# Grouped attention: queries taken transposed from the product, scores over 128 rows of cosine and sine parts, VectorE's bias and maximum ahead of the next tile's rotation

## The reference, cut to what matters

```
def _apply_rope(x, cos, sin):
    x1, x2 = (x[..., :d // 2], x[..., d // 2:])
    c1, c2 = (cos[..., :d // 2], cos[..., d // 2:])
    s1, s2 = (sin[..., :d // 2], sin[..., d // 2:])
    return concatenate([x1 * c1 - x2 * s1, x1 * s2 + x2 * c2], axis=-1)
```

## Time and profile before

| | us |
|---|---|
| time, median of 3 runs (lowest to highest) | 1008.42 (1007.82 to 1012.86) |
| time of the profiled execution | 1005.3 |
| its span, first to last instruction | 1003.5 |
| TensorE busy | 899.9 (90%) |
| VectorE busy | 669.8 (67%) |
| ScalarE busy | 420.8 (42%) |
| GpSimd busy | 375.3 (37%) |
| mean granted clock of TensorE | 0.968 |

### The profile page before, as it was taken

How to read it: one execution, slowest core, us unless ns; L and a number is a source line. 1 busy time by engine, 2 the same in 40 slices (tenths; PEclk the granted TensorE clock), 3 DMA queues, 4 the chain that set the end, 5 groups by cost and what they waited for, 6 DMA issues and landing times. The chain is left out here.

```text
span 1003.5 us, 17466 instructions
## 1 busy us (share of the span) xinstructions
PE 899.9 (90%) x5857; PEld 642.7 (64%) x5864; DVE 669.8 (67%) x1572; ACT 420.8 (42%) x1134; POOL 375.3 (37%) x279
## 2 busy tenths in 40 slices
PE   2899989999889995868899979999999949999997
PEld 2687744444478873744378647777777727778786
DVE  5899968889689988876377698787767531222221
ACT  2566641000146555752455336565655512122222
POOL 1776403333476732506545503333333430111111
PEclk9999999999899997987999999999999969999999
DMA  6100079999400007202356392311110149534200
GB/s 210 59 1 0 1 199 306 319 313 311 170 1 1 0 1 190 87 0 92 112 169 203 91 332 73 112 54 51 51 51 26 43 157 318 190 110 141 93 12 20
DMA packets 87259, 117.17 MB, mean 117 GB/s; under 512 B 12464, under 2 KB 75949, under 8 KB 86781
## 3 DMA queue, kind: packets, MB, share of 16 engines
q1 hardware_dynamic: 77455, 88.15, 29.1%
q10 hardware_dynamic: 4408, 15.46, 4.4%
q0 software_dynamic: 5328, 12.70, 3.5%
HBM read 68.08 MB, written 50.16 MB: 118 GB/s over the span
## 5 line engine op out<-in xcount | busy, mean ns | idle before, releaser
L1016 PE MATMUL psum<-m_W,lnT 128*128 128x512 f32 x256 | 114.2, 598 | 0.7 <-DVE acc L928 0.7
L410 POOL TENSOR_TENSOR prob<-prob,a_rden 128x1232 f32<-128x1232 f32 x30 | 67.5, 2249 | 58.4 <-DVE a_rden L506 58.4
L1016 PEld LDWEIGHTS psum<-m_W,lnT 128*128 128x128 f32 x256 | 47.2, 190 | 59.0 <-issue 56.5
L2907 ACT ACTIVATE prob<-psum,x_b 128x320 f32<-128x320 f32 x64 | 33.7, 527 | 117.1 <-PE psum L2963 117.1
L2574 PE MATMUL psum<-g_VW,pT 128*128 128x256 f32 (+1 forms) x320 | 72.5, 382 | 1.6 <-ACT pT L2461 1.5
L1001 POOL TENSOR_TENSOR m_masked<-m_rel,m_mrow 128x1232 f32<-128x1232 f32 x16 | 41.8, 2614 | 82.9 <-DMA masked_bias<-m_masked 62.0
L2769 POOL DMA_INDIRECT out_x<-x_yt,x_X x20 | 19.8, 991 | 135.3 <-DVE x_yt L2846 135.3
L2574 PEld LDWEIGHTS psum<-g_VW,pT 128*128 128x128 f32 (+1 forms) x320 | 59.5, 190 | 11.2 <-issue 3.7
L2232 POOL TENSOR_TENSOR g_qr<-g_t 128x1024 f32<-128x1024 f32 x15 | 35.4, 2359 | 71.1 <-DVE g_t L2305 71.1
L2239 POOL TENSOR_TENSOR prob<-prob,g_rden 128x1232 f32<-128x1232 f32 x15 | 33.7, 2247 | 67.6 <-DVE g_rden L2340 67.6
L2524 PE MATMUL psum<-g_Wq,lnT 128*128 128x512 f32 x128 | 58.0, 596 | 0.7 <-ACT lnT L2435 0.7
(11 more groups left out here) (464 smaller groups left out, 2235.6 us busy)
## 6 DMA issues: line engine op xcount, KB each, us to landing
routed_rows<-hole SPq DMA_DIRECT2D x8, 2210.0 KB, 33.5
masked_bias<-m_masked ACTq DMA_DIRECT2D x16, 616.0 KB, 7.5
g_bias<-masked_bias SPq DMA_DIRECT2D x16, 616.0 KB, 3.8
m_xb<-routed_rows SPq DMA_DIRECT2D x39, 130.0 KB
m_rel<-in_rel_bias ACTq DMA_DIRECT2D x8, 616.0 KB, 9.6
expert_rows<-hole SPq DMA_DIRECT2D x1, 4680.0 KB, 32.4
g_early_w<-in_L_ffn_w SPq DMA_DIRECT2D x8, 512.0 KB, 4.6
g_early_w<-in_L_ffn_w SPq DMA_DIRECT2D x4, 1024.0 KB, 5.9
```

The source lines that it names most:

```text
L410: nc.gpsimd.tensor_tensor(heads(c.prob[b]), heads(c.prob[b]), rden[b][:, :].unsqueeze(2).to_broadcast([P, H, SK]), ALU.mult).then_inc(norm ...
L1016: last = nt.matmul(c.ps[p][:, :], c.lnT[b][:, k * P:(k + 1) * P], W[:, k, p * 512:(p + 1) * 512], start=(k == 0), stop=(k == KC - 1))
```

## The change

*Queries.* The weights are now the stationary operand and the normalized tile the moving one: 16 matmuls of 128 columns, and the queries come out transposed, the 128 numbers of two heads in the rows and the tokens in the columns. Neither `q_transpose` nor `qT_copy` is left.

*Rotation.* VectorE multiplies the transposed queries with tables (`turn`) whose rows are the 64 numbers of a head and whose columns are positions. Cosine part and sine part aren't added: they are put in the two halves of 128 rows of `turned`, one block of 128 columns for each head. Four instructions of 64 rows, two of which write to the other half of the rows than they read.

*Scores.* One matmul a head, over all 128 rows, so that the contraction adds the two parts: the moving operand `KB` has the keys in rows 0 to 63 and the keys with their halves exchanged in rows 64 to 127, 77 columns, without zeros.

*Softmax.* The maximum is taken in two halves of 8 heads; the exponentials of all 16 heads are single ones with their sums, so the shift and the sums on VectorE are gone. GpSimd's addition is gone.

*Orders.* VectorE: shift(t) now stands ahead of rope(t+1). TensorE: output is cut into three parts among the transposes; `lnT(t+3)` instead of t+2; two banks for the probabilities' transposes; queries of tile 1 in banks 5 and 6, all others in 3 and 4. The additions of experts' results, layer norms' groups, and router pieces stand at other tiles (`COLLECT_AT`, `VARIANCE_AT`, `NORM_GROUPS`). Three small transfers come later in SP's queue.

```
-    c.gC, c.gSn = sb(c, "g_cos", [P, S // P, DH]), sb(c, "g_sin", [P, S // P, DH])
-    c.gKB = sb(c, "g_KB", [P, B, G, 2, SK])
+    c.gC, c.gSn = sb(c, "g_cos", [P, DH]), sb(c, "g_sin", [P, DH])
+    c.gTurn = [sb(c, f"g_turn{u}", [P, S]) for u in range(2)]
+    c.gKB = sb(c, "g_KB", [P, B, G, SK])
...
         def rope(i, u):
+            q = c.psall[:, q_bank(i) * 512:q_bank(i) * 512 + 1024].rearrange("p (m n) -> p m n", n=P)
+            to = turned[i % 2][:, :].rearrange("p (m u n) -> p m u n", u=2, n=P)
+            n0 = i % HALF * P
+            own, other = slice(u * DH, (u + 1) * DH), slice((1 - u) * DH, (2 - u) * DH)
+            if u == 0:
+                dve.wait_ge(s["q_ps"], i + 1)
+                wait(dve, s["s_ps"], i - 1)
+            for rows_, table in ((own, turn[0]), (other, turn[1])):
+                last = nv.tensor_tensor(to[rows_, :, u, :], q[own, :, :],
+                                        table[own, n0:n0 + P].unsqueeze(1).to_broadcast([DH, HB // 2, P]), ALU.mult)
+            if u == 1:
+                last.then_inc(s["roped"], 1)
...
         def shift(t):
+            dve.wait_ge(s["added"], t + 1)
+            nv.reduce_max(mx[b][:, halves[0]], p[:, halves[0]], AX, negate=True).then_inc(s["mx_ok"], 1)
             dve.wait_ge(s["s_used"], t + 1)
-            links(nv.reduce_max(c.mx[:, :], p, AX, negate=True))
-            nv.tensor_tensor(p[:, plain], p[:, plain], c.mx[:, plain].unsqueeze(2).to_broadcast([P, HB - FUSED, SK]),
-                             ALU.add).then_inc(s["shifted"], 1)
+            nv.reduce_max(mx[b][:, halves[1]], p[:, halves[1]], AX, negate=True).then_inc(s["mx_ok"], 1)
...
+        for t in range(NT - 1):
+            if t == HALF + 1:
+                centred()
+            if t in (4, 8):
+                inverse(NORM_OF[t + 3])
+            shift(t)
+            rope(t + 1, 0)
+            rope(t + 1, 1)
             route(t)
+            if t > 0:
+                finished(t - 1)
+            collect(t)
+            places(t)
+            divisors(t)
...
         def queries(i):
             pe.wait_ge(s["lnT_ok"], i + 1)
+            if i >= 2:
+                pe.wait_ge(s["roped"], 1 if i == 2 else i)
+            for m in range(HB // 2):
+                to = c.psall[:, q_bank(i) * 512 + m * P:q_bank(i) * 512 + (m + 1) * P]
                 for k in range(KC):
+                    last = nt.matmul(to, Wq[:, k, m * P:(m + 1) * P], c.lnT[i % 2][:, k * P:(k + 1) * P],
+                                     start=(k == 0), stop=(k == KC - 1))
...
         def scores(t):
+            pe.wait_ge(s["roped"], t + 1)
             wait(pe, s["s_used"], t)
-            for m in range(HB // 2):
+            for h in range(HB):
+                o = h // HPB * 512 + h % HPB * SK
+                last = nt.matmul(c.psall[:, o:o + SK], turned[t % 2][:, h * P:(h + 1) * P], KB[:, t // HALF, h // G, :],
...
+            if t > 0:
+                prob_transpose(t - 1, 0)
+                prob_transpose(t - 1, 1)
+                output(t - 1, 0)
+                prob_transpose(t - 1, 2)
+                if t < NT:
+                    route(t)
+                output(t - 1, 1)
+                if 2 <= t and t + 3 < NT:
+                    lnT(t + 3)
+                output(t - 1, 2)
+                back(t)
+                if t + 2 < NT:
+                    queries(t + 2)
```

More of the change, by code:

```diff
@@ L2098, in _ @@
         for b in range(B):
[L2099 removed]
+            pe.wait_ge(s["kr_ok"], 3 * (b + 1))
             for g in range(G):
@@ L2330, in residual, with divisors @@
-        def residual(i, b):
+            nv.reduce_max(mx[b][:, halves[1]], p[:, halves[1]], AX, negate=True).then_inc(s["mx_ok"], 1)
+        def divisors(t):
+            b = t % 2
+            wait(dve, s["p_ok"], t - 1)
+            dve.wait_ge(s["exp_ok"], t + 1)
+            nv.reciprocal(rden[b][:, :], den[b][:, :]).then_inc(s["rd_ok"], 1)
+            if t == NT - 1:
+                p = heads(c.prob[b])
+                dve.wait_ge(s["rd_ok"], t + 1)
+                for h in halves:
+                    nv.tensor_tensor(p[:, h], p[:, h], rden[b][:, h].unsqueeze(2).to_broadcast([P, HB // 2, SK]),
+                                     ALU.mult).then_inc(s["p_last"], 1)
@@ L2475, in route @@
                 logits_copy(c, r, 0, c.ps[0]).then_inc(s["r_lgT_ok"], 1)
-        def step(t, q):
-            b = q % 2
+        deviation(0)
+        layer_norm(0)
+        lnT_copy(0)
+        deviation(1)
+        na.activation(spare[:, :], c.ones[:, 0:1], ACT.Exp)
+        for i in range(1, 4):
+            layer_norm(i)
+            lnT_copy(i)
+        for t in range(NT):
             if t == HALF + 7:
@@ L2566, in output @@
-        def output(i, b):
-            if i == 0:
-                pe.wait_ge(s["r_rw_ok"], KC)
-            wait(pe, s["x_ok"], i)
-            for j in range(NB):
-                if j % 4 == 0:
-                    pe.wait_ge(s["pT_ok"], i * 3 + (j // 4 + 1))
-                w = P if j < NB - 1 else LASTB
-                last = nt.matmul(bank_y[:, 0:D], c.pT[b][0:w, j * P:(j + 1) * P], VW[0:w, i // HALF, j, :],
+            if i == NT - 1 and u < 2:
+                pe.wait_ge(s["p_last"], u + 1)
@@ new lines, in prob_transpose @@
+            if u == 0:
+                wait(pe, s["pT_ok"], i * 3)
+            elif u == 1:
+                pe.wait_ge(s["lnT_ok"], min(i + 4, NT))
+            else:
+                pe.wait_ge(s["pT_ok"], i * 3 + 1)
+            for j in range(4 * u, min(4 * u + 4, NB)):
+                w = P if j < NB - 1 else LASTB
+                last = nt.transpose(ring[u % 2][0:w, (j % 4) * P:(j % 4 + 1) * P],
+                                    c.prob[i % 2][:, j * P:j * P + w], c.ident[:, :])
+            last.then_inc(s["pT_ps"], 1)
@@ L2575, in output @@
+        def output(i, u):
+            if u == 0:
+                wait(pe, s["x_ok"], i)
+            pe.wait_ge(s["pT_ok"], i * 3 + (u + 1))
+            for j in range(4 * u, min(4 * u + 4, NB)):
+                w = P if j < NB - 1 else LASTB
+                last = nt.matmul(bank_y[:, 0:D], c.pT[i % 2][0:w, j * P:(j + 1) * P], VW[0:w, i // HALF, j, :],
                                  start=(j == 0), stop=(j == NB - 1))
-            last.then_inc(s["y_ps"], 1)
+            if u == 2:
+                last.then_inc(s["y_ps"], 1)
@@ L2609, in banks_read @@
                 pe.wait_ge(s["r_pre_read"], 1)
-        def step(t, q):
-            b = q % 2
+        lnT(0)
+        queries(0)
+        lnT(1)
+        queries(1)
+        lnT(2)
+        for t in range(NT + 1):
             banks_read(t)
-            if inside(t):
-                scores(t, b)
+            if t < NT:
+                scores(t)
             if t == 0:
-                pe.wait_ge(s["r_w_in"], 16)
-                for k in range(KC):
-                    last = nt.matmul(bank_y[:, 0:RW], c.ones[:, :], r.rw[:, k, :], start=(k == 0), stop=(k == KC - 1))
-                last.then_inc(s["r_sum_ps"], 1)
-            if t == HALF + 7:
+                queries(2)
+                lnT(3)
+            if t == NT - 1:
                 pe.wait_ge(s["r_lnT_ok"], ROUTED[2][0])
                 pe_logits(c, r, 1, c.ps[3]).then_inc(s["r_lg_ps"], 1)
+                pe.wait_ge(s["pT_ok"], (NT - 2) * 3)
+                keep_warm(c, ring[0], 6)
             if t == NT:
```

418 lines of the change are left out of this document (168 added, 250 removed).

## The result

The changed kernel takes 1060.52 us (median of 4 runs, 1058.03 to 1064.84) beside 1008.49 us (1007.82 to 1012.86) for the kernel before: a ratio of 1.0511, 95% interval 1.0465 to 1.0557. The direction and most of the 52 us were forecast; the time lies 15.5 us above the 1045 and just outside the range. The profiled execution has a span of 1057.8 us, 54.3 more than the earlier trace rows.

What follows compares the result with a forecast made beforehand. A serial TensorE-VectorE loop was to bind, 15.2 us a tile against 12.9: scores(15) 32.0 us later, +1.6 for that block, +3 at the end, +37 on 1005.3, 1042; plus 3.1 to the median, 1045 us, range 1022 to 1060.

Steps and rivals of the forecast that it cites:

- TensorE's passes: TensorE per tile: queries 32 passes, 3.65 us (+0.2); scores 32 passes of 77 columns at 0.117 us, 3.74 us (+1.64).
- The rival of serial loads and passes: Queries and scores: weight loads and passes don't overlap, 7.0 and 5.6 us a tile, 83 us more, 1128 us; chance 0.02.
- VectorE's half-height instructions: Rotation on VectorE: 64-row instructions cost the same as 128-row ones, 1.14 us start to start; four take 4.65 us.
- The ring: Serial loop per tile: scores, VectorE's bias, maxima and next tile's rotation, then TensorE's queries; 15.2 us against 12.9.
- bias with maxima: VectorE between scores and rotation: bias 1.03 + 0.50 us, maxima 0.70 + 0.70 us, 2.93 us together.
- the hand-over back: From the end of VectorE's rotation to the start of TensorE's next queries: 0.05 us.
- the first rival: The ring doesn't bind; TensorE's own 13.8 us do, 1.4 us a tile less, 20 us less: 1025 us; chance 0.08.
- The clock: Attention stage: granted clock stays at 1.00 (2.4 GHz) despite TensorE's idle time; priced at nothing.
- The start: First tiles: rotation of tile 0 from about 585.24, scores(0) at about 591.5, scores(1) at 603.1, then 15.2 us a tile.
- The end: From scores(15): the block itself +1.6 us; last output done 17.5 us after the scores instead of 14.4, +3 us.

Runs made afterwards that it cites:

- the run with the missed terms mended: Changed kernel with unused TensorE passes before scores(1) and the last transposes, lnT(4) behind scores(2), router copies ahead of exponentials: 1047.2 us, ratio 1.0383.
- the first: Changed kernel with VectorE's rotation of tile t+1 put ahead of bias and maximum of tile t: 1051.7 us, ratio 1.0380.
- the second: Changed kernel with TensorE issuing scores(t+1) ahead of queries(t+2) from tile 2 on: 1080.4 us, ratio 1.0640.
- the third: Changed kernel with rotation ahead of bias and maximum, third probabilities copy ahead of exponentials, four groups of unused TensorE passes: 1047.2 us, ratio 1.0391.

## Why the prediction missed

*TensorE's passes: right.* Queries 3.65 us, as worked out. Scores 3.53 us from start to start (703.34 to 706.87), 0.110 us a pass of 77 columns, where I took 0.117 from 32 columns. A pass of 128 columns costs 0.114 us (3.65 / 32): the price hardly depends on the columns here, as it would if the load of 128 columns set the pace. The rival of serial loads and passes, 5.6 us for the scores, is contradicted: no block at full clock took more than 3.84 us.

*VectorE's half-height instructions: right.* 1219 ns in the mean over 64 of them (1204 to 1228), half of which write to the other 64 rows. The run with only the queries transposed has both heights side by side: 1223 ns for 128 rows, 1226 and 1218 for 64. Between them the starts lie 1.23 us apart and not 1.14: 4.92 us in place of 4.65.

*The ring: right.* 15.27 us for the 15.2 forecast. That it is so close is in part luck: scores were 0.21 us shorter and bias with maxima 0.11, the rotation 0.27 and the hand-over back 0.10 longer. The sum also priced the last step, which has no queries, like the others; it took 13.00 us. The two runs with a product inside and outside show that it is this loop that binds, and the run with the rotation first that TensorE's own work, 13.38 us, comes next; the first rival's step was right for the plain steps of that run, and its 20 us were too many for the kernel, which got some 13.

*The clock: the step that failed.* "I cost it at nothing" held for the plain steps, with 1.65 us of wait in each. It did not hold at the stage's ends, where the waits are longer. I had no row for it, took one stretch of the attention before as covering the whole stage, and named the clock among the things that would break the forecast without asking where TensorE would wait longest. My own working had that place: scores(1) wait for all of VectorE's part, which came out at 11.6 us of step with 3.74 of scores and 3.65 of queries in it. That is 4 us of wait, and the same 32 passes then took 7.11 us. By the starts it cost 3.4 us there, 2.0 at scores(2) and 2.9 at scores(15), and the last output and the next part's start ran at it too. The first run with passes without use shows the cause: with the wait filled, the clock stayed at 1.00 and 5.3 us of the schedule were gone.

*The start: missed a wait.* Scores(0) came at 591.65 for 591.5, though the rotation of tile 0 began at 586.67 and not at 585.24. I priced the step from tile 1 to 2 as a plain one. In the written order `lnT(4)` stands ahead of scores(2), and tile 4 opens a norm group. 21.7 us in place of 15.2, of which 3.4 are the clock in scores(1); the run with `lnT(4)` behind scores(2) has 18.7.

*The end: +3 us, too small.* From scores(15) on it was +11.9 us, forecast 1.6 + 3. The banks' readers were not followed: scores(15) wait 2.81 us for the router's copies behind ScalarE's exponentials. Against the sum that wait itself cost nothing, since the step with it was 2.2 us shorter than the 15.2 priced; what it cost is the half clock behind it. In the run with the missed terms mended this stretch is 25.3 us long, +5.8, which leaves the forecast 1.2 us short.

The profiled execution's miss of 17.7 us (54.3 less the 36.6 forecast) adds up by the starts: scores(1) 0.2, the next step 6.5, the one behind it 2.1, the eleven plain and router steps 1.2, the last step -2.2, the end 7.3, the next part 2.7.

The mended run, 1.0383, is 12.8 thousandths or 13 us under the changed kernel, with some 6 us to either side: of the 15.5 us of error these terms are about 13, and the rest is within the scatter. How the 13 us divide among clock, norm group and router isn't settled by times, since they feed each other (a wait removed also removes the half clock behind it); by the start times it is 5.3 for the passes at the start, and 5.1 for the norm group's order with the half clock behind it; together the four edits took 9.1 us between scores(1) and scores(15).

## What to carry to other kernels

When two engines hand a tile to and fro, add up the loop through both queues, not each engine's busy time; here it was good to 0.1 us in 15, with single terms off by up to 0.3. Then look at where the loop is not yet, or no longer, in its rhythm, and price the longest wait of TensorE there twice: once as a wait, once as half clock behind it. And before cutting such a loop, list what its slack hides; three cuts here brought the plain steps to 13.4 us, which over 11 steps should save 21 us. The kernel got some 13 us from the first, a loss from the second, and some 12 us from the third, which had passes against the half clock as well.

## What was not expected of the hardware

Waits of 0.23 to 1.65 us ahead of the queries, one in every tile of 15.3 us, left the granted clock at 1.00 from 645 to 815 us; in the run with the product in the ring, waits of 2.0 to 2.6 us lost it in nine of ten tiles and for different lengths (5.44 or 6.76 us in place of 3.81 for the same 32 passes).

One VectorE instruction of 128x3 elements, which takes 0.16 us elsewhere, took 2.01 us:

```profile
621.79 0.18 DVE L2272 RECIPROCAL rstd<-std 128x3 f32<-128x3 f32 x1
622.00 2.01 DVE L2273 SCALAR_TENSOR_TENSOR g_shifts<-mean,rstd 128x3 f32<-128x3 f32 x1
```

GpSimd was multiplying the probabilities at that time (from 621.75, 2.25 us). The traces bear this out beyond the one case. In the stage this instruction ran 70 times in all 14 traces: 30 times it began inside that product of GpSimd and took 0.87 to 2.02 us, ending each time within 0.03 us of the product's end, and 40 times it began elsewhere and took 0.16. It also goes the other way: in the run with the product outside the ring, VectorE's product began 0.16 us ahead of GpSimd's in 13 tiles, and GpSimd's then took 2.83 us in place of 2.25. Not every instruction is held, as the reciprocal of 0.18 us shows. In the kernel before, this one never fell on GpSimd's product, but four other small ones of the norm groups did, and took 1.51 to 2.16 us there. No run moved them apart, so what it is worth in either kernel is open; where it showed it was 0.78 us of ScalarE's wait at the start of the changed kernel and, as an estimate, 1.7 us in one step of the run with the rotation first.
